# Three tiny loads on ScalarE's DMA queue, ahead of the small inputs of a conditioned residual layer

## What is computed

```python
q_emb = relu(q @ W3 + b3)                      # 64 x 1024
v_sum = sum(v, axis=1, keepdims=True)          # over the 128 tokens
x2    = (n * v + v_sum) * q_emb[:, None, :]    # n = 128
out   = v + relu(x2 @ W2 + b2)
```

## Time and profile before

| | us |
|---|---|
| median of 3 executions | 638.76 |
| lowest, highest | 638.45, 639.19 |
| the profiled execution, own time | 638.39 |
| its span, first to last instruction | 636.6 |
| PE busy | 630.6 (99%) |
| ACT busy | 421.7 (66%) |
| DVE busy | 443.4 (70%) |
| POOL busy | 16.7 (3%) |

### The profile page before, as it was taken

How to read it: one execution, slowest core, us unless ns; L and a number is a source line. 1 busy time by engine, 2 the same in 40 slices (tenths; PEclk the granted TensorE clock), 3 DMA queues, 4 the chain that set the end, 5 groups by cost and what they waited for, 6 DMA issues and landing times.

```text
span 636.6 us, 9267 instructions
## 1 busy us (share of the span) xinstructions
PE 630.6 (99%) x2799; PEld 519.0 (82%) x2799; DVE 443.4 (70%) x670; ACT 421.7 (66%) x902; POOL 16.7 (3%) x21
## 2 busy tenths in 40 slices
PE   9999999999999999999999999999999999999997
PEld 6888778888888888888888888888888888888886
DVE  3888979676876758677576776758677576776533
ACT  4879696939568494865939567494865939577320
POOL 1530000000000000000000000000000000000000
PEclk9999999999999999999999999999999999999999
DMA  9935465543363643437353353643446353350703
GB/s 302 407 126 195 164 236 196 203 168 119 158 214 132 201 167 133 158 143 253 132 185 117 155 202 132 234 155 127 143 160 235 132 195 124 150 191 0 251 12 132
DMA packets 27518, 108.83 MB, mean 171 GB/s; under 512 B 3056, under 2 KB 3184, under 8 KB 23664
## 3 DMA queue, kind: packets, MB, share of 16 engines
q1 hardware_dynamic: 27360, 108.54, 47.4%
q10 hardware_dynamic: 144, 0.14, 0.1%
HBM read 75.11 MB, written 33.55 MB: 171 GB/s over the span
## 4 chain that ended last, share of the span: by engine, by line
PE 87%; ACT 6%; DVE 5%; issue 1%; POOL 0%; ACTq 0%; DVEq 0%
PE acc L283 87%; ACT x_sb L399 3%; ACT w_hi L418 2%; DVE w_lo L661 1%; DVE vsum L593 1%; DVE a_lo L656 1%; ACT acc L470 1%; PE acc L300 1%; DVE xn L669 0%; ACT a_hi L381 0%; POOL x_sb L568 0%; ACT a_hi L394 0%; DVE w_stage L665 0%; DVE x_sb L641 0%; ACT q_emb L466 0%
## 5 line engine op out<-in xcount | busy, mean ns | idle before, releaser
L283 PE MATMUL acc<-w_hi,a_hi 128*128 128x512 f32 x904 | 352.4, 390 | 1.5 <-issue 0.9
L283 PE MATMUL acc<-w_hi,a_lo 128*128 128x512 f32 x904 | 351.7, 389 | 0.0
L283 PE MATMUL acc<-w_lo,a_hi 128*128 128x512 f32 x904 | 351.7, 389 | 0.0
L399 ACT ACTIVATE x_sb<-x_sb,bias,scale 128x128 f32<-128x128 f32 x496 | 205.9, 490 | 14.0 <-DVE bias L601 14.0
L283 PEld LDWEIGHTS acc<-w_hi,a_hi 128*128 128x128 f32 x904 | 169.7, 188 | 39.1 <-issue 2.8
L283 PEld LDWEIGHTS acc<-w_hi,a_lo 128*128 128x128 f32 x904 | 169.7, 188 | 35.4
L283 PEld LDWEIGHTS acc<-w_lo,a_hi 128*128 128x128 f32 x904 | 169.7, 188 | 34.8
L656 DVE TENSOR_TENSOR a_lo<-x_sb,a_hi 128x512 fp32r<-128x512 f32 x150 | 103.5, 690 | 106.3 <-ACT a_hi L394 105.5
L394 ACT CAST a_hi<-x_sb 128x512 fp32r<-128x512 f32 x150 | 93.6, 624 | 38.8 <-PE acc L283 37.6
L394 ACT CAST a_hi<-s 128x512 fp32r<-128x512 f32 x60 | 37.4, 624 | 72.0 <-PE acc L283 69.0
L593 DVE TENSOR_REDUCE vsum<-x_sb 128x16 f32<-128x2048 f32 (+1 forms) x38 | 73.8, 1943 | 8.0 <-DMA x_sb<-x_t 8.0
(11 more groups left out here) (46 smaller groups left out, 193.1 us busy)
## 6 DMA issues: line engine op xcount, KB each, us to landing
xn<-x SPq DMA_DIRECT2D x64, 512.0 KB, 4.0
out<-xn SPq DMA_DIRECT2D x62, 512.0 KB, 3.8
x_sb<-x_t SPq DMA_DIRECT2D x30, 1024.0 KB, 4.9
x_sb<-w_t SPq DMA_DIRECT2D x8, 256.0 KB, 5.9
x_sb<-x_t SPq DMA_DIRECT2D x8, 256.0 KB, 7.3
u_sb<-w_q SPq DMA_DIRECT2D x3, 512.0 KB, 8.2
m_sb<-w_q SPq DMA_DIRECT2D x3, 512.0 KB, 9.0
w_stage<-w_q SPq DMA_DIRECT2D x4, 256.0 KB, 6.3
```

The lines of the kernel that those rows point to most:

```text
L283: return nc.tensor.matmul(dst, lhs, rhs, start=False, stop=False, skip_group_check=True)
L399: last = nc.scalar.activation(x_sb[:, slot, t, k], x_sb[:, slot, t, k], ACT.Identity, bias=bias[:, slot, t, k:k + 1], scale=scale[:, slot, ...
```

## The change

The change allots a small buffer `touch_sb` (16 partitions, 3 x 16 words) and a semaphore `touched`. At the head of ACT's program, ahead of the load of `small_t`, three loads are issued into it: the first 16 words of every eighth row of `x_t[0]` (16 rows), the first 16 words of every eighth row of the first quarter of W2 (16 rows), and the first 16 words of `b2`. The copy of `b_first` into bank 2, after the four pieces of B11 are rounded, also waits for the three loads. Nothing reads the buffer. The loads of the same tensors on SP's queue stay as they are.

```diff
+        touch_sb = sb("touch_sb", [P // 8, 3, 16])
...
-        small_loaded = sem("small_loaded")
+        small_loaded, touched = sem("small_loaded"), sem("touched")
...
+            first_tokens = x_t[0].rearrange("(r s) t k n -> s r (t k n)", s=8)
+            first_w = w2_q[0, 0].rearrange("(r s) m -> s r m", s=8)
+            act.dma_start(touch_sb[:, 0], first_tokens[0, :, :16]).then_inc(touched, 16)
+            act.dma_start(touch_sb[:, 1], first_w[0, :, :16]).then_inc(touched, 16)
+            act.dma_start(touch_sb[0:1, 2], b2[:, :16]).then_inc(touched, 16)
             act.dma_start(small_sb[:], small_t).then_inc(small_loaded, 16)
             act.wait_ge(table_set, 1)
...
                 cast_w("b11", k, b11_loaded[k], 16)
             act.wait_ge(marked, 1)
+            act.wait_ge(touched, 48)
             seed_plain(2, b_first)
```

## The result

| | kernel before | changed kernel |
|---|---|---|
| median of 4 executions, us | 638.61 | 647.71 |
| lowest, highest | 638.38, 639.19 | 646.87, 648.08 |
| ratio (95% interval) | | 1.0128 (1.0104 to 1.0152) |
| own time of the profiled execution | 638.39 | 647.80 |
| its span | 636.6 | 646.0 |

The forecast was 639.5 us, with a range up to 641.2. The loss is 9.1 us, twelve times the forecast one; between the two profiled executions it is 9.4 us, and the first block product starts 7.9 us later. The kernel before was also run beside the experiments, 59 times: 53 of these executions took 637.97 to 640.02 us and 6 took 643.59 to 644.25 us, which no trace here explains, so a median over few executions is to be read with this in mind.

What follows compares the result with a forecast made beforehand. PE was taken to bound the kernel, with the start fully on its path. Issues of 1.36 us less 0.60 us of lower clock gave 0.76 us, plus 0 for wait and earlier data: 638.76 + 0.76 = 639.5 us, range 638.4 to 641.2.

Steps and rivals of the forecast that it cites:

- What bounds the kernel: Whole kernel: PE busy 99% of the span, no room after the start, so the start is worth all its length.
- The issues: ACT's queue ahead of `small_t`: three tiny loads at 0.45 us each, 1.36 us in all, bounds 0.2 and 1.8 us.
- The time to landing: Load of `small_t` at the start: 3.5 us from issue as before, landing at 5.60 us; upper bound 4.0 to 5.3 us.
- The clock: PE's start: clock rises late after idling, each slow `q_sum` costing 0.60 us; 640.1 to 642.5 us, middle 641.2; chance 0.16.
- two rivals: At the start: `small_t` much later, 640.0 to 641.3 us, chance 0.12; clock late, middle 641.2 us, chance 0.16.
- The sum's own step: First `q_sum` from 5.60 us at the higher clock lasts 0.94 us, so only 0.76 of 1.36 us reach the path.
- The engines and PE move together, and that stall is as long as before: From first block product to PE's 1.31 us stall at 66.44 us: the 0.76 us shift stays, stall unchanged.
- What the tiny loads may give: DMA dip at 5 to 7 us, read as first-access price: data up to 0.95 us sooner; gain taken as 0.
- The added wait: Before the copy at about 13 us: the three loads have landed by 6 us, so it costs nothing.

Runs made afterwards that it cites:

- PE kept at work: Changed kernel with 13 more matmuls on zeros on PE between the first eight and the wait for `small_t`: 644.15 us, ratio 1.0063.
- SyncE held back: Changed kernel with SyncE waiting for `small_t` after W3's first four pieces, before issuing the first tokens and what follows: 645.15 us, ratio 1.0091.
- PE held back alone: Kernel before, loads untouched, with PE waiting for the first tokens before its first `q_sum`: 648.73 us, ratio 1.0143.
- four kernels with pauses of 1.46 to 2.88 us: Changed kernel with SyncE held back (645.15 us), single-row loads (645.32) or POOL's second subtraction delayed (646.00); kernel before with `small_t`'s issue awaiting PE's second matmul (646.27).

## Why the prediction was wrong, point by point

**What bounds the kernel: the start, right; "whatever moves its first block product moves the end by as much", not so.** 6.99 of the 9.44 us come from the start. But the first block product moved by 7.9 us and the end by 9.4 us, and in two experiments by 3.4 and 5.8 us (PE kept at work) and by 4.4 and 3.2 us (SyncE held back). What lies between, ACT, DVE and POOL up to 66 us, can add or take back some us.

**The issues: right.** 0.42, 0.44 and 0.53 us; `small_t` at 2.22 us, for 2.10 forecast.

**The time to landing: the step that failed first.** It was taken as the 3.5 us of before, with 5.3 us as the upper bound, and measured 5.88 us. The argument for 3.5 was that W3's fourth piece took its 5.3 us because of its own queue. The runs speak for the other reading: around 5 to 7 us the DMA stream falls to 150 to 300 GB/s, and what is under way then is late, W3's fourth piece and `small_t` alike. Issued by 1.2 us, `small_t` took 3.2 to 3.9 us and landed ahead of that stretch; issued at 1.84 to 2.27 us beside the full stream it took 4.3 to 6.5 us. The dip stood in the earlier trace rows, but it was weighed only as a possible gain.

**The clock: right as a rival, wrong in its price.** It was given 0.16 and priced for a landing at 5.6 us, with a highest case of 642.5 us. The late landing and the lost clock were set up as two rivals with a chance each. They are one case: the later `small_t` lands, the longer PE idles, and the idle is what costs the clock. PE held back alone reproduces the whole (648.7 us), PE kept at work takes 3.6 us off. The sum's own step, a `q_sum` at the higher clock after the idle (0.94 us forecast), failed: it lasted 1.55 us (weight loads from 8.15 to the next group's at 9.70 us), and the `q_sum`s came 2.03 us apart, 0.98 us more than at the higher clock, where the rival had 0.60 + 0.2 us. In the four kernels with pauses of 1.46 to 2.88 us the first `q_sum` was fast, but the clock fell behind it. The `q_sum`s themselves, 7.8 us of them, did not raise it; it rose during the eleven matmuls on zeros behind them.

**"The engines and PE move together, and that stall is as long as before": wrong.** ACT and DVE did move together by 6.99 us for 30 us. But POOL's first subtraction had hung on a DMA (its wait of 8.65 us in the kernel before was for `u_sb`), and that load's landing moved by 2.9 us only. Relative to DVE POOL came 1.4 us sooner with its first subtraction and 0.6 us sooner with its second (39.69 and 46.13 us), which was enough to be ahead of an instruction with two inputs. That cost 1.7 us, by which PE's stall is longer (2.98 for 1.31 us), and 0.7 us for the second fall of the clock behind it. The Trainium skill has the rule, "SBUF — State Buffer", section "Who interferes with whom": a `tensor_tensor` of the vector engine with both inputs in SBUF contends with a GpSimd operation that reads SBUF, and the second to issue is fully blocked. The traces agree: 2.41 us for 0.16, POOL's own 3.26 us for 2.41 where DVE was first, and a reduction with one input beside the same subtraction not held up (2.27 us).

**What the tiny loads may give: 0, right; its ground, wrong.** Issued behind `small_t` they cost and gain nothing (1.0002). But the dip isn't the price of first accesses to these three tensors: in the changed kernel the last of the tiny loads had landed at 4.13 us, and the dip came all the same, at 203 and 228 GB/s up to 6 us; and `small_t` was as late when they read only `small_t`. (They read 16 of 128 rows; a price of each row's first access would not be covered by this.) What makes it is open: it needs the loads that follow W3 (376 GB/s without them), and not the one of `b2`.

**The added wait: 0, right.** The three loads had landed 16 us before the copy that waits for them (20.31 us). That copy came at 13.33 us before.

## What to carry to other kernels

A load that the first matmuls wait for belongs at the head of its queue; what is put ahead of it is priced not by its own issue time alone but by the traffic into which the load then falls. Where a late start lets TensorE idle, ask what the lower clock costs in all that follows until it rises again, and treat the two as one case. And when engines move by some microseconds, look for the one whose work hangs on a DMA: it need not move with them, and may then meet another engine where the two hold each other up.

## What the runs showed of the hardware that was not expected

- A DMA issue on ACT went out at 1.21 us, while the table load of the activation ahead of it ran from 0.74 us and the activation itself came at 2.03 us.
- An issue of 16 rows costs as much as one of 128 (0.42 to 0.44 us against 0.41). A load of a single row cost 0.53 us behind these two; of three such loads in a row the first cost 0.52 us, the others 0.21 and 0.27 us.
- The granted clock stayed at 0.50 through the 7.8 us of the four `q_sum`s in the changed kernel (8.15 to 15.99 us) and came back to 1.00 only during the matmuls on zeros behind them (0.50 from 16 to 18 us, 0.83 on average from 18 to 19 us).
- A pause of PE of 1.5 to 2.9 us right after the start did not slow the first `q_sum` behind it (0.97 us), but the clock fell to 0.50 between 7.9 and 8.8 us, during the second or just behind it.
- Somewhere between 4 and 8 us the DMA stream falls to 150 to 300 GB/s for a microsecond or two in every kernel here that issues the tokens and B11 right behind W3; where these go out from 6.2 us on, it falls to 197 GB/s at 9 to 10 us.
